# A four-layer graph network: edge tiles with a carry row, rounded mask products, and new places for row transfers and fills

## The reference

```python
def gat_conv(x, src, dst, W, a_src, a_dst, bias):      # layer 0, twice, with a loop at each node
    h = (x @ W).reshape(n, 4, 256)
    e = leaky_relu((h * a_src).sum(-1)[src] + (h * a_dst).sum(-1)[dst], 0.2)
    w = exp(e - segment_max(e, dst)[dst])
    alpha = w / segment_sum(w, dst)[dst]
    return segment_sum(h[src] * alpha, dst) + bias      # relu after each, then @ Wfc + bfc
relu(segment_sum((h @ weight)[src] * edge_weight, dst))  # layer 1, "conv"
# layer 2, "painn": a filter product per edge, segment_sum over src, three small products
segment_sum(relu(concat(x[src], x[dst]) @ W.T + b), src)  # layer 3, "mlp"
```

## Time and profile before

| | us |
|---|---|
| runs | 2660.74, 2663.48, 2661.98 |
| median | 2661.98 |
| profiled execution, its own time | 2663.84 |
| its span | 2662.1 |
| TensorE busy | 2472.9 |
| VectorE busy | 1582.8 |
| GpSimd busy | 1041.3 |
| ScalarE busy | 1004.9 |

### The profile page before, as it was taken

How to read it: one execution, slowest core, us unless ns; L and a number is a source line. 1 busy time by engine, 2 the same in 40 slices (tenths; PEclk the granted TensorE clock), 3 DMA queues, 4 the chain that set the end, 5 groups by cost and what they waited for, 6 DMA issues and landing times. The chain is left out here.

```text
span 2662.1 us, 35707 instructions
## 1 busy us (share of the span) xinstructions
PE 2472.9 (93%) x11306; PEld 1957.0 (74%) x11306; DVE 1582.8 (59%) x4824; ACT 1004.9 (38%) x1823; POOL 1041.3 (39%) x1007
## 2 busy tenths in 40 slices
PE   6999999699999999999999999999999788684897
PEld 5878888588778888888777888878888545462575
DVE  7767777446663344425453227888888678264675
ACT  5951122223443222223343225555544324352243
POOL 2056374442224573062221104565454362550232
PEclk8999999899999999999999999999999889796799
DMA  5348565335664222224665325666544275443331
GB/s 180 142 138 132 178 198 164 125 95 172 213 221 144 82 88 96 96 76 158 225 214 176 115 100 182 198 198 202 170 160 167 78 238 180 141 153 127 107 97 64
DMA packets 179492, 398.47 MB, mean 150 GB/s; under 512 B 52505, under 2 KB 81412, under 8 KB 178404
## 3 DMA queue, kind: packets, MB, share of 16 engines
q1 hardware_dynamic: 113792, 211.80, 23.5%
q0 software_dynamic: 65552, 184.85, 23.0%
HBM read 226.17 MB, written 170.41 MB: 149 GB/s over the span
## 5 line engine op out<-in xcount | busy, mean ns | idle before, releaser
L1434 PE MATMUL g_h_ps<-held_w_hi,g_x_hi 128*128 128x512 f32 x1264 | 524.2, 415 | 2.6 <-DVE g_x_lo L1555 2.6
L1436 PE MATMUL g_h_ps<-held_w_hi,g_x_lo 128*128 128x512 f32 x1264 | 494.7, 391 | 0.0
L1435 PE MATMUL g_h_ps<-held_w_lo,g_x_hi 128*128 128x512 f32 x1264 | 493.4, 390 | 0.0
L1469 ACT ACTIVATE g_act_t<-g_t_ps,g_b_col 128x256 f32<-128x256 f32 (+1 forms) x640 | 260.8, 468 | 367.4 <-PE g_t_ps L1408 367.2
L564 DVE CUSTOM_DVE_ANT_0 g_prod<-g_h_sb,g_a_rows 128x256 f32<-128x256 f32 x632 | 225.0, 420 | 94.2 <-ACT g_h_sb L462 91.4
L1434 PEld LDWEIGHTS g_h_ps<-held_w_hi,g_x_hi 128*128 128x128 f32 x1264 | 238.0, 188 | 55.4 <-issue 9.6
L1435 PEld LDWEIGHTS g_h_ps<-held_w_lo,g_x_hi 128*128 128x128 f32 x1264 | 238.4, 189 | 52.8 <-issue 9.6
L1482 ACT ACTIVATE g_h_sb<-g_h_ps 128x512 f32<-128x512 f32 x158 | 94.5, 598 | 482.7 <-PE g_h_ps L1436 482.6
L1436 PEld LDWEIGHTS g_h_ps<-held_w_hi,g_x_lo 128*128 128x128 f32 x1264 | 237.5, 188 | 51.3
L1553 DVE CAST g_x_hi<-g_act_t 128x512 fp32r<-128x512 f32 (+1 forms) x320 | 161.5, 505 | 188.7 <-ACT g_act_t L1469 187.4
L1434 PE MATMUL g_h_ps<-fc_w_hi,g_x_hi 128*128 128x512 f32 x632 | 264.1, 418 | 0.1
(11 more groups left out here) (402 smaller groups left out, 4484.5 us busy)
## 6 DMA issues: line engine op xcount, KB each, us to landing
h<-g_h_sb SPq DMA_DIRECT2D x158, 512.0 KB, 2.7
g_x_in<-h SPq DMA_DIRECT2D x59, 512.0 KB, 4.2
g_x_in<-in_dram SPq DMA_DIRECT2D x40, 512.0 KB, 5.0
h<-g_rows SPq DMA_DIRECT2D x40, 512.0 KB, 3.2
x<-fc_x SPq DMA_DIRECT2D x20, 512.0 KB, 4.8
x<-conv_x SPq DMA_DIRECT2D x20, 512.0 KB, 3.2
x<-painn_normed SPq DMA_DIRECT2D x20, 512.0 KB
g_w_raw<-in_dram SPq DMA_DIRECT2D x12, 512.0 KB, 5.4
```

The lines of the kernel that those rows point to most:

```text
L1434: pe.matmul(out, xh, wh, start=(k == 0), stop=False)
L1435: pe.matmul(out, xh, wl, start=False, stop=False)
L1436: last = pe.matmul(out, xl, wh, start=False, stop=(k == KC - 1))
L1469: last = act.activation(act_t[:, k, 0:width], t_ps[f % 2][:, c, 0:width], ACT.Relu, bias=b_col[:, m // GM, k:k + 1])
```

## The change

An edge tile now holds 127 edges in rows 1 to 127; row 0 is the carry row. An edge's place in the table is its rank plus the number of full tiles ahead of it plus 1 (four more VectorE steps). After a tile's product, row 0 of its sums is the running sum of the tile's last node; ScalarE copies that one row into row 0 of the next tile's messages, so that one mask and one product do what two did. In conv, painn and mlp the second product, the second mask and the `last_row` constants go, and the one-row copy comes.

In the node layers the mask is 0 or 1 and kept in the rounded format for all 20 tiles (made in the first layer, used in both). The source rows are multiplied by their weights and split into two rounded parts: ScalarE the high (`round_src`), VectorE the low (`split_src`); the carry row likewise (`round_carry`, `split_carry`). `add_up` is four rounded products of 512 columns and one unrounded one of 4. ScalarE scales the sums (`share_sums`), VectorE adds the own row. Source rows have two buffers instead of three.

The pace is two edge tiles per three half tiles: halves 21 to 49 and 119 to 147. The order of node tiles changes (ten of the A tiles, ten early B tiles, the rest), the fc weights are loaded at each half from 150 (before: each second from 134), and the fills of a four-half macro stand after k = 2 and 6 of its first two halves.

The key rows are written by five transfers on SP instead of two on POOL: the `srt` tiles from SBUF, and 20 words each from the record tables. `scan_row` is a new row for the scan over the keys. The sorted records are read after a small copy in DRAM that fills each tile's row 0 (`heads`), and a third load per table (`head`) fetches that row once more.

```diff
@@ dense_and_prep, SP
+                sp.wait_ge(first_set, 1)
+                for o, (rec_in, row_out) in enumerate(((rec_d, row_d), (rec_s, row_s))):
+                    last_keys = by_place(rec_in[P - 1:P - 1 + EP])[0:1, :, 0:1].rearrange("p t k -> p (t k)")
+                    sp.dma_start(in_row(row_out)[1:P, :], srt[o][1:P, :, 0],
+                                   allow_slow_non_contiguous=True).then_inc(rows_out, 16)
+                    sp.dma_start(in_row(row_out)[0:1, :], last_keys, allow_slow_non_contiguous=True).then_inc(rows_out, 16)
+                sp.dma_start(in_row(scan_row[1:EP + 1]), srt[0][:, :, 0],
+                               allow_slow_non_contiguous=True).then_inc(rows_out, 16)
                 loop(W2_FROM - 2, W2_FROM)
...
@@ dense_and_prep, GpSimd
                     pool.wait_ge(scattered[o], 16 * ET)
-                    pool.dma_start(srt[o][:, :, :], rec_in[0:EP].rearrange("(t p) k -> p t k", p=P)).then_inc(sorted_in, 16)
-                    pool.dma_start(nxt[o][:, :, :], rec_in[1:EP + 1].rearrange("(t p) k -> p t k", p=P)).then_inc(sorted_in, 16)
-                for rec_in, row_out in ((rec_d, row_d), (rec_s, row_s)):
-                    pool.dma_start(row_out[1:EP + 1], rec_in[0:EP, 0:1].rearrange("a b -> (a b)"),
-                                   allow_slow_non_contiguous=True).then_inc(rows_out, 16)
+                    heads = [rec_in[n:n + EP + P].rearrange("(t p) k -> p t k", p=P)[0] for n in range(2)]
+                    pool.dma_start(heads[0], heads[1]).then_inc(headed[o], 16)
+                for o, rec_in in enumerate((rec_d, rec_s)):
+                    pool.wait_ge(headed[o], 16)
+                    pool.dma_start(srt[o][:, :, :], by_place(rec_in[0:EP])).then_inc(sorted_in, 16)
+                    pool.dma_start(nxt[o][:, :, :], by_place(rec_in[1:EP + 1])).then_inc(sorted_in, 16)
+                    pool.dma_start(head[:, o, 1:ET, :], by_place(rec_in[P - 1:P - 1 + EP])[0:1, 0:ET - 1, :]).then_inc(sorted_in, 16)
...
@@ EdgeSums, TensorE
     def add_up(self, pe, t):
...
-        for hd in range(H):
-            cols = slice(hd * C, (hd + 1) * C)
-            pe.matmul(h.sum_ps[:, cols], m[:, hd, :], h.h_src[t % RING][:, cols],
-                      start=(hd % 2 == 0), stop=False, skip_group_check=True)
-        pe.matmul(h.misc_ps[:, 0:H], m[:, H, :], self.weights(t, 0), start=True, stop=False)
-        pe.matmul(h.misc_ps[:, 0:H], m[:, H + 1, :], prev[:, HC:HC + H], start=False, stop=True)
+            pe.wait_ge(self.carry_lo, t)
+            pe.wait_ge(self.sums_out, t)
+        mask = h.mask[:, t * P:(t + 1) * P]
         for n in range(2):
-            last = pe.matmul(h.sum_ps[:, n * 512:(n + 1) * 512], m[:, H + 1, :], prev[:, n * 512:(n + 1) * 512],
-                             start=False, stop=True, skip_group_check=True)
-        last.then_inc(self.summed, 1)
+            cols = slice(n * 512, (n + 1) * 512)
+            pe.matmul(h.sum_ps[:, cols], mask, h.src_hi[q][:, cols], start=True, stop=False)
+            pe.matmul(h.sum_ps[:, cols], mask, h.src_lo[q][:, cols], start=False, stop=True)
+        pe.matmul(h.misc_ps[:, 0:H], mask.bitcast(F32), self.weights(t, 0),
+                  start=True, stop=True).then_inc(self.summed, 1)
...
@@ EdgeSums, ScalarE and VectorE (new)
+    def round_src(self, act, t):
...
+            last = act.activation(h.src_hi[q][:, cols], h.h_src[q][:, cols], ACT.Copy,
+                                  scale=self.weights(t, 0)[:, hd:hd + 1])
+    def round_carry(self, act, t):
...
+        act.activation(h.src_hi[1 - q][0:1, :], h.sum_ps[0:1, :], ACT.Copy).then_inc(self.carry_hi, 1)
+    def share_sums(self, act, t):
...
+            last = act.activation(h.sums[:, cols], h.sum_ps[:, cols], ACT.Copy, scale=h.rden[:, q, hd:hd + 1])
+    def split_src(self, dve, t):
...
+            last = dve.scalar_tensor_tensor(h.src_lo[q][:, cols], h.h_src[q][:, cols],
+                                            self.weights(t, 0)[:, hd:hd + 1],
+                                            h.src_hi[q][:, cols].bitcast(F32), ALU.mult, ALU.subtract)
+    def split_carry(self, dve, t):
...
+        dve.tensor_tensor(h.src_lo[1 - q][0:1, :], h.sum_ps[0:1, :], h.src_hi[1 - q][0:1, :].bitcast(F32),
+                          ALU.subtract).then_inc(self.carry_lo, 1)
...
@@ node_layers
-    EARLY_B = 6
-    order = [*range(A_TILES), *range(ENDS, ENDS + EARLY_B), *range(A_TILES, ENDS), *range(ENDS + EARLY_B, TILES)]
+    EARLY_A, EARLY_B = 10, 10
+    order = [*range(EARLY_A), *range(ENDS, ENDS + EARLY_B), *range(EARLY_A, ENDS), *range(ENDS + EARLY_B, TILES)]
...
-    at1 = {SUMS1 + t: t for t in range(ET)}
-    at2 = {SUMS2 + t: t for t in range(ET)}
-    WFC = SUMS2 + ET + 3
+    paced = lambda t: 3 * (t // 2) + t % 2
+    SPAN = paced(ET - 1) + 1
+    at1 = {SUMS1 + paced(t): t for t in range(ET)}
+    at2 = {SUMS2 + paced(t): t for t in range(ET)}
+    WFC = SUMS2 + SPAN + 2
...
+        slow = halves_done(m) - first_half[m] == 4
+        return [(k, f) for i, k, f in (((0, 2, 0), (0, 6, 1), (1, 2, 2), (1, 6, 3)) if slow else
+                                       ((0, 0, 0), (0, 2, 1), (0, 4, 2), (0, 6, 3))) if first_half[m] + i == h]
...
@@ mlp_edges, TensorE (conv_edges and painn_edges alike)
-                    pe.matmul(sum_ps[q][:, :], mask[q][:, 0, :], msg[q][:, :], start=True, stop=False)
-                    pe.wait_ge(sums_out, t + 2)
-                    pe.matmul(sum_ps[q][:, :], mask[q][:, 1, :], sums[1 - q][:, :], start=False, stop=True).then_inc(summed, 1)
+                    pe.wait_ge(carried, t + 1)
+                    pe.matmul(sum_ps[q][:, :], mask[q][:, :], msg[q][:, :], start=True, stop=True).then_inc(summed, 1)
```

More of the change, by code:

```diff
@@ L227, in dense_and_prep @@
         CONST = 8
+        by_place = lambda rows: rows.rearrange("(t p) k -> p t k", p=P)
+        in_row = lambda row: row.rearrange("(t p) -> p t", p=P)
         def first(i):
@@ L660, in use_factors @@
                     last.then_inc(u_done, 1)
-                dve.wait_ge(sorted_in, 64)
+                dve.wait_ge(sorted_in, 16 * 6)
                 settle()
+                step(dve.memset(head[:, 0, 1:ET, 4:5], 1.0))
+                settle()
+                for o in range(2):
+                    step(dve.tensor_copy(srt[o][0:1, 1:ET, :], head[:, o, 1:ET, :]))
+                settle()
+                dve.sem_inc(first_set, 1)
                 for o in range(2):
@@ L839, in gather_src @@
     def gather_src(self, pool, t):
-        h, s = self.hold, t % RING
-        if t >= RING:
-            pool.wait_ge(self.summed, t - RING + 1)
+        h, s = self.hold, t % 2
+        if t >= 2:
+            pool.wait_ge(self.src_lo, t - 1)
         pool.indirect_dma_start(h.h_src[s][:, :], None, self.h_rows[0:self.rows], h.index(t, self.src)).then_inc(self.src_in[s], 16)
@@ L1438, in products @@
                             last.then_inc(tile_done, 1)
-                        if h == first_half[m] and m + 1 < MACROS and k % 2 == 0:
-                            fill(m + 1, k // 2)
+                        for after, f in fills(h):
+                            if k == after:
+                                fill(m + 1, f)
                 def edges(e, at, score, h):
@@ L1905, in _, with copy_sums @@
                 act.preload_act_table_set("natural_log_exp_and_others")
-                def copy_sums(i, s):
+                def copy_sums(i, s, last=False):
                     t = RING * i + s
                     act.wait_ge(summed, t + 3)
+                    if not (last and s == RING - 1):
+                        after = x_src[0:1, bass.ds((t + 1) * D, D)]
+                        act.wait_ge(x_in[(s + 1) % RING], 32 * (i + 1 + (s + 1) // RING))
+                        act.activation(after, sum_ps[s % 2][0:1, :], ACT.Copy).then_inc(carried, 1)
                     act.wait_ge(turned, t + 1)
@@ L2320, in copy_sums, with carry @@
                     act.activation(sums[s % 2][:, :], sum_ps[:, :], ACT.Copy).then_inc(sums_out, 1)
+                def carry(i, s):
+                    t = RING * i + s
+                    act.wait_ge(msg_done, 3 * t + 4)
+                    act.wait_ge(summed, t + 1)
+                    act.activation(msg[0:1, :], sum_ps[0:1, :], ACT.Copy).then_inc(carried, 1)
                 def copy_sums_t(i, s):
@@ L2403, in _ @@
                     dve.sem_inc(done, 1)
-                dve.memset(keys[:, 0:1], -5.0)
-                for s in range(2):
-                    dve.memset(sums[s][:, :], 0.0).then_inc(zeroed, 1)
                 def masks(i, s):
@@ L2662, in sum_edges @@
                     pe.wait_ge(sums_out, t + 1)
[L2663 to L2668 removed]
+                    pe.wait_ge(carried, t + 1)
+                    pe.matmul(sum_ps[q][:, :], mask[q][:, :], msg[q][:, :], start=True, stop=True).then_inc(summed, 1)
+                pe.sem_inc(carried, 1)
                 turn(0, 0)
@@ L2741, in body @@
```

(4 more changed lines are left out.)

434 lines of the change are left out of this document (229 added, 205 removed).

## The result

| runs of one session | before | after |
|---|---|---|
| median, us | 2661.36 (2659.78 to 2663.48) | 2635.04 (2631.99 to 2635.59) |
| profiled execution, span, us | 2662.1 | 2633.2 |

The ratio is 0.9898, 95% interval 0.9881 to 0.9915: 26 us faster. The forecast was 57 us faster, so less than half of it came.

What follows compares the result with a forecast made beforehand. PE was taken as the bound, busy 93% of the span and full in the node layers. Savings of 137, +5 for sorting and +75 for row transfers gave -57 from 2663.84, forecast 2605 us, range 2530 to 2715.

Steps and rivals of the forecast that it cites:

- The sums of an edge tile in the node layers: Node layers: each add_up falls from 3.93 to 1.2 us, 109 us saved over 40 tiles; node layers -106 in all.
- The carry chain: Node layers: ACT and DVE prepare the next add_up's carry row in some 4.8 of 5.44 us, costed at nothing.
- rival 3: Node layers: carry work does not fit into 5.44 us; 1 us late costs 20, giving 2625 us; chance 0.10.
- the 0 to 7 added for them: Start of the fc products: seven late weight roundings stand behind the relus feeding PE; 3 us added, between 0 and 7.
- Fills spread over halves 0 and 1: 0: Node layers: the fills' work is the same and PE waits for them nowhere in the full window; 0 us.
- The five row transfers: Dense stage, SP's queue: 5080 runs on one engine at 15 ns, 76 us; PE stands 71 us; +75 with slow clock.
- sign of a DMA share near 1/16: Dense stage, profile after: DMA share near 1/16 during PE's wait of about 71 us for x near 313 us.
- Rival 1: Row transfers: rows dealt over all 16 engines, or runs nearly free; 0 to +12 us, time 2533 us; chance 0.14.
- Rival 2: Row transfers: one engine and dear 4-byte DRAM writes; 35 ns a run gives 2707 us, slower than before; chance 0.31.
- The sorting chain: Before the dense products: loads wait for a DRAM copy of heads, plus small steps; +5 us (0 to 10).
- The three edge stages: Conv, painn and mlp: removed second products and masks save 5, 8 and 17 us, and 1 at their starts.
- the forecast -8: Painn: second sum product gone ahead of ACT's copy, 0.54 us for some 15 of 20 tiles; -8 us (4 to 11).

Runs made afterwards that it cites:

- the second profile: The kernel before, unchanged, executed once more on the chip of the other runs; measured 2663.28 us.

## Why the prediction was right in part

- **The sums of an edge tile in the node layers** held: -106 forecast, -104.6 measured, products 0.23 us apart, PE full. The carry chain fits, even at one tile per half; rival 3 is out. The 2.2 us for the fc weights lie inside the 0 to 7 added for them. "Fills spread over halves 0 and 1: 0" had the right sum with a wrong reason: the fills would have cost 4.6 us had they stayed, so their cover was thin.
- **The five row transfers** held in mechanism: the runs of 127 partitions go one after another, and 67.2 us of wait came where 71 was forecast. That the size fits so well is in part luck: a run took 12.0 ns and not 15, and `scan_row`, which was to hide beside, cost most of the 10 us that this left. The forecast's sign of a DMA share near 1/16 failed: it was 0.12. Rival 1 is out for 127 partitions, and dear even where it holds: dealt over 16 engines the rows cost 21.1 us, not 0 to 12. Rival 2 is out: in one line of writes a run takes 12.0 ns, not 26 or more.
- **The sorting chain** held: +5 forecast, +4 to +9 with the rows out of the way, and PE's wait near 235 us, 7.45 where it was 1.16 (2.36 in the second profile), is at the place named.
- **The three edge stages** is the step that failed, and it is the whole miss: -31 forecast with the starts, +1.6 measured. It priced the removed products by their duration where PE looked full, and costed the one-row copies at nothing without naming their cover. In mlp the size was right and the cover was not: the carry copy stands ahead of the sums copy, 13 of 17 us went there, and came back when the two were exchanged. In conv the product lay in the shadow of DVE's split; 5 was taken from one mask, of which the tiles gave 2.2 and the stage's start and end took 1.8 back. In painn 0.54 a tile became 0.15 in late tiles, at full clock the carry chain held the early ones at 5.2 to 5.3 us where they could run at 4.35, and the clock stayed low for longer, which with the rest of those early tiles cost 9 us in after and less in other profiles; without the carry the stage was 10 us below before, near the forecast -8. What keeps the clock low stays open.
- Two slips of the working change nothing: DVE's steps of a tile add up to 5.7 us and not 5.5, and the runs are 7680 and not 7660.

The best version, turned rows, the order in mlp, one pace, and the carry of painn on DVE, takes 0.955 of before: 120 us faster where the change as made was 26 us faster. Of the 94 between them, by the stages of the two profiles, 70 lie in the dense stage (the row transfers), 13 in mlp (the order), 3 in the node layers (the pace), 6 in painn and 2 in conv; the 6 are within what painn's stage varies by.

## What to carry to other kernels

A transfer's partition count can decide its time more than its bytes: 127 rows were written one run after another on SP's queue, and whatever stands behind them in the same queue waits; cut them to 112 and 15, or turn the data so that a run is some 100 bytes. When a product is removed, ask for the loop that sets the period, not for the busy share of its engine: a product in another engine's shadow is worth nothing. And each small copy that a change adds has a place in a queue: put it, and the wait that it needs, behind the one that somebody waits for.

## What the runs showed of the hardware

- SP is held at an issue for 30.39 us when a transfer of 127 partitions with 2540 runs stands ahead of it; cut into 112 and 15 partitions, for 0.82 us.
- Runs of 4 bytes to neighbouring words cost 12.0 ns each in one line of writes, and 54 ns for each engine when 16 write at once (3.4 ns a run together); with 64 bytes from word to word 1.6 ns together (one profile).
- The same kernel took 2661 to 2663 us on two chips and 2936 on a third, where PE and ACT idle without a releaser that the profile shows (one wait of ACT of 36.28 us).
- The clock's rise after a wait is no constant: 10 to 50 us at the lower level (granted clock 0.50) at the start of the same stage with the same code.
